# Three-part scores for every head, new instruction sequences, and four expert blocks moved into the last tail of a decoder layer

## What is computed

```python
q = l2norm(xn @ Wq * 16) * 4;  k = l2norm(xn @ Wk) * 4          # 16 heads of q, one of k and v
x = x + layernorm(softmax(q @ k.T) @ v @ Wout)
state = state * exp(d_t * A) + (d_t * u_t) * B_t;  y_t = sum_n state * C_t
x = x + (y + D * u) * silu(layernorm(x))
for e in range(32):                                             # combine is 0 where e is not used
    g, u = split(xl @ w_gu[e].T);  out += (silu(g) * u) @ w_d[e].T * combine[:, e]
```

## Time and profile before

| | |
|---|---|
| time of the runs | 1514.94 us median of 3 (1511.84 to 1518.72) |
| the profiled execution | 1499.86 us, span 1498.1 us |
| mean granted PE clock | 0.952 of full speed |
| PE / DVE / ACT / POOL busy | 1351.0 / 1098.7 / 936.0 / 475.0 us |
| expert blocks run | 68 |

### The profile page before, as it was taken

How to read it: one execution, slowest core, us unless ns; L and a number is a source line. 1 busy time by engine, 2 the same in 40 slices (tenths; PEclk the granted TensorE clock), 3 DMA queues, 4 the chain that set the end, 5 groups by cost and what they waited for, 6 DMA issues and landing times.

```text
span 1498.1 us, 26182 instructions
## 1 busy us (share of the span) xinstructions
PE 1351.0 (90%) x6762; PEld 992.1 (66%) x6763; DVE 1098.7 (73%) x1513; ACT 936.0 (62%) x2454; POOL 475.0 (32%) x367
## 2 busy tenths in 40 slices
PE   5699899999999999999999999999943779999996
PEld 4367686546888664678865467876422667888885
DVE  3377589849888995988898598887877446766763
ACT  4658785447878645787864578776320446666663
POOL 0000010000021331331133133163412776766674
PEclk9799999989999999999999999999975789999998
DMA  7459997704788771468777136868812469998883
GB/s 237 170 172 260 276 241 179 190 17 115 171 239 200 188 184 36 115 172 240 197 188 187 36 108 170 248 144 207 215 26 91 105 138 236 228 229 222 231 193 53
DMA packets 137515, 256.80 MB, mean 171 GB/s; under 512 B 48717, under 2 KB 50206, under 8 KB 129104
## 3 DMA queue, kind: packets, MB, share of 16 engines
q0 software_dynamic: 36480, 122.30, 36.9%
q1 hardware_dynamic: 76704, 86.70, 19.9%
q10 hardware_dynamic: 24240, 46.68, 9.9%
HBM read 166.37 MB, written 46.21 MB: 142 GB/s over the span
## 4 chain that ended last, share of the span: by engine, by line
PE 61%; DVE 10%; issue 9%; DMA 9%; ACT 6%; DVEq 1%; POOL 1%; ACTq 1%; SPq 1%; POOLq 0%
PE bank L670 12%; PE bank L693 10%; PE bank L653 6%; DMA out<-y_ring,add_ids 3%; PE bank L537 3%; PE pair L614 3%; PE pair L616 3%; PE pair L615 3%; PE pair L537 3%; PE bank L1161 2%; DMA c_bc<-bc_dram 2%; PE bank L655 2%; PE bank L1163 2%; PE bank L1162 2%; DMA y<-state 2%
## 5 line engine op out<-in xcount | busy, mean ns | idle before, releaser
L670 PEld LDWEIGHTS bank<-v_aug,probs 128*128 128x128 f32 x2048 | 237.1, 191 | 22.2 <-ACT probs L1350 16.7
L670 PE MATMUL bank<-v_aug,probs 128*128 128x129 f32 x2048 | 244.2, 275 | 5.1 <-ACT probs L1350 5.1
L2830 POOL DMA_INDIRECT lists<-entry,slot x128 | 199.8, 1561 | 131.7 <-DVE slot L2320 93.9
L693 PE MATMUL bank<-wout,o_t 128*128 128x512 f32 x512 | 233.3, 611 | 5.1 <-issue 4.3
L1359 ACT ACTIVATE decay<-delta,neg_a 128x511 f32<-128x511 f32 x256 | 165.2, 720 | 50.4 <-DVE dbu L2144 31.3
L1350 ACT ACTIVATE probs<-bank 128x512 f32<-128x512 f32 x256 | 153.0, 608 | 63.0 <-PE bank L670 37.6
L693 PEld LDWEIGHTS bank<-wout,o_t 128*128 128x128 f32 x512 | 98.5, 196 | 125.3 <-issue 125.1
L2845 POOL DMA_DIRECT2D y<-dbu x32 | 28.6, 894 | 380.5 <-DVE dbu L2149 271.6
L2144 DVE TENSOR_TENSOR_SCAN dbu<-decay,dbu 128x1024 f32<-128x1024 f32 x64 | 144.6, 2281 | 4.9 <-ACT decay L1359 2.8
L2144 DVE TENSOR_TENSOR_SCAN state<-decay,state 128x1024 f32<-128x1024 f32 x64 | 145.3, 2284 | 2.5
L2939 POOL DMA_INDIRECT out<-y_ring,add_ids x68 | 119.9, 1763 | 77.0 <-DMA out<-y_ring,add_ids 42.2
(11 more groups left out here) (242 smaller groups left out, 2844.7 us busy)
## 6 DMA issues: line engine op xcount, KB each, us to landing
y<-dbu POOLq DMA_DIRECT2D x32, 1024.0 KB
w_raw<-in_w_exp ACTq DMA_DIRECT2D x64, 512.0 KB
wq<-wq_dram POOLq DMA_DIRECT2D x30, 1024.0 KB, 8.6
y<-state POOLq DMA_DIRECT2D x28, 1024.0 KB
wout<-in_wout SPq DMA_DIRECT2D x64, 256.0 KB, 5.0
b_bc<-bc_dram SPq DMA_DIRECT2D x64, 256.0 KB, 4.1
c_bc<-bc_dram SPq DMA_DIRECT2D x64, 256.0 KB, 5.2
lists<-in_const ACTq DMA_DIRECT2D x3, 2904.0 KB, 13.7
```

The lines of the kernel that those rows point to most:

```text
L670: mm = pe.matmul(bank_o[half][:, (t % 2) * (DH + 1):(t % 2 + 1) * (DH + 1)], probs[:, k, t * P:(t + 1) * P], v_aug[:, k, :], start=(k == 0 ...
L693: mm = pe.matmul((bank_o + bank_s)[t][:], o_t[:, h, t * P:(t + 1) * P], wout[:, h % 4, :], start=(h == 0), stop=(h == H - 1))
L2830: pool.indirect_dma_start(out=lists, out_offset=bass.IndirectOffsetOnAxis(ap=slot[:, t, k:k + 1].bitcast(U32), axis=0), in_=entry[:, t, :] ...
```

## The change

There are three parts.

1. Every head is scored in three f32r matmuls. `q_t` and `k_t` are gone, `q_hi` and `q_lo` hold four heads, and DVE makes `q_lo` for each head.
2. The written sequences of all streams in the rows are new: the same calls, with 32 more `q_lows`, in another order.
3. Lists of experts 0 to 3 have their first block closed behind the third row (if fewer than 128 tokens are in it by then, the count is filled up). These four blocks are numbered 0 to 3, the second blocks of the same experts follow from block 4. SP loads their ids (`lists_first`) and POOL gathers their tokens (`get_first`) when `out_proj` of row 3 is done. PE, ACT and DVE work through them by calls written out between the router, the counting steps and the loop. POOL interleaves row 3's sends with the adds and gathers of blocks 0 to 13. Experts 0 and 1, and 2 and 3, then share a loop (`two_experts`), since their remaining blocks count together.

```diff
-                if j < 2:
-                    pe.wait_ge(S["qT_ok"], r * H + h + 1)
-                else:
-                    pe.wait_ge(S["klo_ok"], r + 1)
-                    pe.wait_ge(S["qlo_ok"], r * G * 2 + g * 2 + (j - 1))
+                pe.wait_ge(S["klo_ok"], r + 1)
+                pe.wait_ge(S["qlo_ok"], r * H + h + 1)
...
-                if j < 2:
-                    mm = pe.matmul(bank_s[k % 2][:], k_t[:, tile], q_t[:, j, :], start=True, stop=True)
-                else:
-                    pe.matmul(bank_s[k % 2][:], k_hi[:, tile], q_hi[:, j - 2, :], start=True, stop=False)
-                    pe.matmul(bank_s[k % 2][:], k_lo[:, tile], q_hi[:, j - 2, :], start=False, stop=False)
-                    mm = pe.matmul(bank_s[k % 2][:], k_hi[:, tile], q_lo[:, j - 2, :], start=False, stop=True)
+                pe.matmul(bank_s[k % 2][:], k_hi[:, tile], q_hi[:, j, :], start=True, stop=False)
+                pe.matmul(bank_s[k % 2][:], k_lo[:, tile], q_hi[:, j, :], start=False, stop=False)
+                mm = pe.matmul(bank_s[k % 2][:], k_hi[:, tile], q_lo[:, j, :], start=False, stop=True)
...
-                act.activation(k_t[:], bank_t[1][:], ACT.Copy).then_inc(S["kT_ok"], 1)
...
+            def lists_first():
+
+                sp.wait_ge(S["op_ps"], NB * TT)
+                sp.wait_ge(S["sent"], (NB - 1) * SENT)
+                for r in range(PRE):
+                    load_get(0, r, r * CAP)
+                    load_add(r, r * CAP)
...
+                pe.wait_ge(S["lgs_ok"], NB)
+                gate_up(0, 0, 0)
                 ranks(b)
+                ht(0)
+                counts()
+                down(0, 0)
+                xt(0, 2)
+                table_rows()
+                gate_up(1, 1, 1)
+                ht(1)
...
+                load_expert(3)
                 gates(b)
                 split_expert(2, 0)
+                split_expert(2, 1)
+                split_expert(3, 0)
+                split_expert(3, 1)
                 norm_seed(b, "f")
-                split_expert(2, 1)
+                xt(0)
+                xt(1)
...
+            xt(2)
+            hidden(1)
+            split(2, 0)
+            split_rest(2)
+            ht(1)
+            hidden(2)
+            xt(3)
+            ht(2)
+            split(3, 0)
+            split_rest(3)
+            hidden(3)
+            ht(3)
...
+            sends(0)
+            pool.wait_ge(S["x2_out"], NB * 16)
+            add_next(0)
+            sends(1)
             pool.wait_ge(S["xf_out"], NB * 16)
+            get_now(4)
+            sends(2)
+            add_next(1)
+            get_now(5)
```

More of the change, by code:

```diff
@@ L42 @@
 QUAD = 4
+PRE = 4
 LIST_COLS = NE + 1
@@ new lines, in counts, with table_rows @@
+            def counts():
+                pe.wait_ge(S["carry_ok"], NB)
+                pe.matmul(cnt_bank[:, 0:NE], ones, carry[:], start=True, stop=True).then_inc(S["cnt_ps"], 1)
+            def table_rows():
+                pe.wait_ge(S["cols_ok"], 1)
+                for i in range(6):
+                    row = bank_t[1][0:1, i * P:(i + 1) * P] if i < 4 else bank_t[0][0:1, (i - 4) * P:(i - 3) * P]
+                    mm = pe.matmul(row, cols_f[:, i:i + 1], ident, start=True, stop=True)
+                mm.then_inc(S["rows_ps"], 1)
@@ L745, in ranks @@
                 pe.matmul(bank_t[0][:, 0:TT * NE], ones, carry[:].unsqueeze(1).to_broadcast([P, TT, NE]), start=False, stop=False)
+                if b == NB - 2:
+                    filled = bank_t[0][:, TT * NE:TT * NE + PRE]
+                    pe.matmul(filled, ones, carry[:, 0:PRE], start=False, stop=False)
+                    for t in range(TT):
+                        pe.matmul(filled, ones, r["act"][:, t, 0:PRE], start=False, stop=False)
                 for t in range(TT - 1):
@@ L1142, in _ @@
-            pe.matmul(ht_bank[:, 0:NE], ones, carry[:], start=True, stop=True).then_inc(S["cnt_ps"], 1)
-            pe.wait_ge(S["cols_ok"], 1)
-            for i in range(6):
-                row = bank_t[1][0:1, i * P:(i + 1) * P] if i < 4 else bank_t[0][0:1, (i - 4) * P:(i - 3) * P]
-                mm = pe.matmul(row, cols_f[:, i:i + 1], ident, start=True, stop=True)
-            mm.then_inc(S["rows_ps"], 1)
-            def xt(q, r):
-                wait_apart(pe, S[f"blk_in{r}"], q * 16 + 16)
-                for k in range(KT):
-                    mm = transpose(pair[:, r % 2, k * P:(k + 1) * P], x_blk[:, r, k * P:(k + 1) * P])
-                mm.then_inc(S["xt_ps"], 1)
@@ L1923, in _, with expert_at, two_experts @@
             act.reg_mov(more_now, more_blocks(act, 0))
-            act.reg_mov(blk_now, 0)
-            xt(0)
-            silu(0)
-            xt(1)
-            def expert(e, splits, loads, last=False):
+            act.reg_mov(blk_now, PRE)
+            xt(4)
+            silu(4)
+            xt(5)
+            def expert_at(blk):
+                return act.value_load(blocks[0:1, bass.ds(blk + B_EXPERT, 1)], min_val=0, max_val=PRE - 1)
+            def two_experts(following, opened):
+                more, c = act.snap(more_now, min_val=MIN_BLK - 1, max_val=2 * EXP_BLK), act.snap(blk_now, min_val=0, max_val=MAX_BLK)
+                ht(c)
+                xt(c + 2)
+                for e in opened[0:1]:
+                    split(e, 0)
+                    split(e, 2)
+                silu(c + 1)
+                for e in opened[0:1]:
+                    split(e, 1)
+                then = more_blocks(act, following)
+                with act.Fori(0, more) as k:
+                    blk = c + k
+                    weigh(blk, expert_at(blk))
+                    ht(blk + 1)
+                    xt(blk + 3)
+                    silu(blk + 2)
+                for e in opened[1:]:
+                    split_expert(e, 0)
+                    split_expert(e, 1)
+                act.reg_mov(more_now, then)
+                act.reg_mov(blk_now, c + more + 1)
+                weigh(c + more, expert_at(c + more))
@@ L1930, in expert @@
+            def expert(e, splits, loads, last=False, opened=()):
                 more, c = act.snap(more_now, min_val=MIN_BLK - 1, max_val=EXP_BLK - 1), act.snap(blk_now, min_val=0, max_val=MAX_BLK)
@@ L2964, in _, with get_now, sends @@
+            def get_now(blk):
+                get_next(-1, blk - 2)
+            def sends(k):
+                send_last(range(k, k + 1))
+            pool.wait_ge(S["op_ps"], NB * TT)
+            pool.memset(x_blk[:], 0.0).then_inc(S["blank_ok"], 1)
+            pool.wait_ge(S["blank_ok"], 1)
+            pool.wait_ge(S["xf_out"], (NB - 1) * 16)
+            for r in range(QUAD):
+                get_first(r)
             pool.wait_ge(S["slot_ok"], NB)
             pool.wait_ge(S["entry_ok"], NB * 2)
-            send_last(range(0, 3))
+            sends(0)
@@ new lines, in _ @@
+            sends(2)
+            add_next(1)
+            get_now(5)
+            sends(3)
+            add_next(2)
+            get_now(6)
+            sends(4)
+            get_now(7)
+            add_next(3)
+            sends(5)
+            get_now(8)
+            get_now(9)
+            add_next(4)
+            sends(6)
+            get_now(10)
+            get_now(11)
+            add_next(5)
+            sends(7)
+            get_now(12)
+            get_now(13)
+            add_next(6)
```

1735 lines of the change are left out of this document (912 added, 823 removed).

## The result

Beside the kernel before on the same chip the changed kernel took 1494.57 us (median of 4 runs, 1490.73 to 1497.15) against 1513.39, a ratio of 0.9875 (95% interval 0.984 to 0.9909), or -18.8 us. In a second comparison, of 12 runs, it took 1500.62 against 1507.75, a ratio of 0.9941 (0.9906 to 0.9977), or -9 us (the two medians alone differ by 7.1). The two intervals only just overlap. The middle of the two is a ratio of 0.991, or -14 us. The profiled execution of after took 1492.85 us (span 1491.1), that of before 1499.86, and of this pair the difference is 7.0 us. Executions of one kernel differ by more than that, so a place is read from the traces and a size from the timed runs.

What follows compares the result with a forecast made beforehand. It took PE to bound the rows (874.6 of 900 us busy) and the experts, and DVE's chain the tail. Rows -21, sequences 0 and early blocks -10 gave -31 us, 1514.9 to 1484 us, range 1469 to 1502.

Steps and rivals of the forecast that it cites:

- rival A: Rows: DVE becomes the bound, so the scores bring 8 us or less instead of 21, giving 1497 us; chance 0.15.
- rival B: Tail: POOL's queue makes blocks 4 to 11 wait as long as now, part 3 brings 0, giving 1494 us; chance 0.16.
- PE's 7 us per row: Scores in the rows: three f32r matmuls save PE 0.22 us per call over 128 calls, 28 us in all.
- the net of -21: Rows: of PE's 28 us, 4 are lost at row 3's end and 3 to new small waits, leaving -21 us.
- so about 19 remain: DVE in a row: about 31 us of slack, less 7 for the shorter row and 5.4 of new `q_lows`.
- Part 2, at 0: New sequences in the rows: the same calls, taken as 0 beyond part 1; at most PE's 25 idle us to win.
- Rival C: Rows: added `q_lo` stand behind scan pieces while PE waits, making the kernel slower, +42 us, 1557 us; chance 0.06.
- Part 3, -10 us: Tail and experts: four early blocks bring -12.7 us, less +1.4 for late gates and +1.3 for expert openings.
- So this queue sets when the blocks up to 10 can run: POOL's queue in the tail: its shortening brings the gather of block 10 12.7 us earlier, at 59.0 us after 1147.7.
- The term of +1.4: ACT in the tail: three weight-load issues ahead of `gates` take 1.44 us and delay what is queued behind them.
- the openings: Blocks 8 to 10: splitting weights of experts 4, 5 and 6 leaves DVE no slack against PE, costing +1.3 us.
- the three signs: Wrong if `x_blk`/`w_lo` waits in blocks 4 to 11 exceed 8 us, gates slip over 2, or `out_stats` waits for scan.

Runs made afterwards that it cites:

- order_only: The kernel before with only the new sequences of the first row and rows 0 to 2, scoring as before: 0.9953 of before, 1501.02 us.
- rows_new: The kernel before with part 1 and the new sequences of the first row and rows 0 to 2, last row, tail and experts unchanged: 0.9897 of before, 1492.04 us.
- the nine profiles: Profiles of nine kernels, after among them, with the same code for the first row and rows 1 and 2: row 1 took 260.0 to 265.5 us.
- the cut sends: The changed kernel, and before with only the new rows, each without 9 of row 3's 32 sends: 0.9816 and 0.9776 of before.
- spread: The changed kernel with shared-expert loops written out and experts 4, 5 and 6 opened one by one: 0.9919 of before, 1498.97 us.
- after_again: The changed kernel run once more beside the partial kernels on the same chip: 0.9941 of before, 1500.62 us.
- straight: The changed kernel with the loops of `two_experts` on ACT and DVE written out for this routing: 0.9898 of before, 1495.16 us.
- rows_last: The changed kernel without part 3, all new sequences kept, including the last row's: 0.992 of before, 1497.89 us.
- two_parts: The changed kernel without the third matmul of each score call, `q_lo` still computed: 0.9808 of before, 1483.18 us.
- cut_after: The changed kernel without 9 of row 3's 32 sends and their list entries: 0.9816 of before, 1482.76 us.
- double_qlo: The changed kernel with each of the 32 added `q_lo` computed twice on DVE: 0.9991 of before, 1509.31 us.
- scores_only: The kernel before with part 1 in before's sequences, added `q_lows` placed by hand and `key_lo` moved ahead: 1.024 of before, 1542.5 us.

## Why the prediction was only partly right

The direction and the range held, the size did not: -31 us forecast, some -14 measured. That the range held was partly luck. Rivals A and B came true together. By my own prices that is 1514.9 - 8 = 1507, outside the range that I gave. The 7 us below it came from a term that I had put at nothing, the new order.

**Part 1, PE's 7 us per row: right.** PE's busy time fell by 7.2 us in row 0 (`order_only` to `rows_new`) and by 7.2 and 4.2 in rows 1 and 2 (before to after). The granted clock was 0.98 and 0.99 in these two rows of before, 0.99 and 0.98 in after, so the 7.2 of row 1 are read a little high and the 4.2 of row 2 low.

**Part 1, the net of -21: wrong, rival A, and this is the first step that failed.** From `order_only` to `rows_new` part 1 brought 8 us (known to some 8), which is what rival A gave it. The step is "so about 19 remain. DVE's new work is therefore covered, but only by slack that is scattered." I had counted only the softplus wait (17.5 us) as fixed and the other 31 us of DVE's idle time as slack. The runs show that some 37 us per row are not to be had, even with 14.7 us less for PE. Before had 45, so only about 8 were there, and the added `q_lo` took some 4 to 5 of them. Row 0 gave its 7 us, and rows 1 and 2 gave 4.2 and 0.8, with the order's small share in it. Row 3 and the tail gave less than nothing: from the `scan_in` of row 3 to the first send before took 1147.68 - 823.9 = 323.8 us, after 1133.52 - 806.5 = 327.0, and in the nine profiles of the same rows 322.0 to 333.9. I had warned that DVE would be late there and took 4 us off. The wait for PE's `out_proj` went from 5.9 to 0.9 us, so it is the scan's stream that now ends last there.

**Part 2, at 0: wrong by 7 us alone, and by far more as a step.** The orders filled row 0's idle time (-5.5 us to the first `scan_in`, ratio 0.9953, interval 0.9917 to 0.999). And part 1 is a loss of 36 us in before's order. The two parts can't be costed one at a time. Rival C named such a loss and I gave it 0.06 because the new order was there to prevent it. That reason was sound, but then the order is worth what it prevents. The other reason, that PE never waited over 1.1 us for anything in the rows of before, was a misreading of the earlier trace rows. The 1.1 us belong to the largest group alone, and the views of the same window have single waits of up to 1.8 us:

```profile
PE bank L653 <- ACT probs L1350: 2.0, 2, 1.8
```

**Part 3, -10 us: wrong, rival B.** The step that failed is "So this queue sets when the blocks up to 10 can run", as I used it. The queue has a hand in the pace, as the cut sends show (as far as their lighter blocks don't explain it). But I followed it only to the gather of block 10 and forecast 59.0 us behind the first send; it came at 65.6. The sum had one wait in it, 2.4 us at the gather of block 4. There were two large ones, 5.3 us there and 4.8 at the add of block 4. And I took a gain at that point for a gain of the run. The queue as a whole still held 32 sends and 8 adds, only four gathers had left it, and its waits rose: idle time before sends, gathers and adds, without the wait for the slots, is 9.5 + 8.8 + 11.7 = 30.0 us, against 9.5 + 6.6 + 6.1 = 22.2. Adds now stand between more of the sends, and one of them, of block 4, waits 4.8 us for its ids. I had also let the early blocks fit into PE's idle time ahead of the table, where only the first of them ran. So the add of block 7 stayed at 85.0 (83.2), and from there both kernels have 60 blocks to go. The rest of the span is this number times the pitch: (1484.31 - 1218.52) / 60 = 4.43 us in after. The term of +1.4 for `load_expert(3)` ahead of `gates` was right. ACT in after, the issues and the first instruction of `gates`, which stood directly behind the same step in before:

```profile
1095.66 1.44 ACTq L1439 DMA_DIRECT2D w_raw<-in_w_exp  x3
1097.13 1.28 ACT L1423 ACT_TABLE_LOAD   x1 [1.33 <-issue]
```

`rows_new`, with before's ACT order there, reached the first send at 1133.51, no earlier than after, but its router's matmuls ran at a granted clock of 0.50 and took 6.9 us, against 3.8 at 0.93 in after. For the openings I had +1.3. `spread`, which takes them apart, won nothing, so no run shows this term.

**What I had said would make me wrong.** Of the three signs one came up clearly: `out_stats` hardly waits for PE any more. The gates start 1.3 us later behind the weight loads, within the 2 us. PE's waits for `x_blk` and `w_lo` from block 4 on are 0.9 us in after (1167 to 1272 us) and 8.3 us in `after_again` (1174 to 1274 us), just over the limit of 8. The sign was badly chosen. The waits for `w_lo` came earlier, at the early blocks (7.4 us in after), and behind them PE waited for other things: for `ht_lo` 8.5 us in after, 1.7 in before (1180 to 1285 us). Of what I had expected to see, the row windows were to be 5 to 7 us shorter each, the gather of block 10 some 11 us earlier and four `down` ahead of the table. They were 4.2 and 0.8, 6.2, and one.

**What stays open.** In the profiles of after, `straight` and `rows_last`, and less so of `spread`, `two_parts` and `cut_after`, ACT stands idle for 4 to 8 us several times among blocks 4 to 10, with nothing of this kernel in the trace to wait for (in after between 1176 and 1217 us); in those of `after_again` and `rows_new` it doesn't. It comes with before's tail too, so it isn't part 3's. The Trainium skill, Runtime: NRT & Kernel Launch, section Instruction fetch mechanics, says that a taken branch out of the fetched window stalls an engine. The code without loops had the idle time all the same, and only one packet of each instruction queue lies between 1176 and 1217 us in after, so these runs don't bear out that cause. The cause stays open, and so does that of the lower clock behind block 7.

## What to carry to other kernels

Idle time of an engine isn't slack until something has used it. Take work away from the engine that is called the bound, and add some to the next: here 59 us less on PE brought 15, 21 more on DVE cost 12, and with the windows of single rows that showed whose chain set the pace. Count the instructions that an edit really takes out, in the trace. Cost an edit together with the order that it needs, since the same calls gained 16 us in one order and lost 36 in another. And where a queue feeds a stretch, compare where the whole queue ends, not where one of its items comes; here work that was taken out behind it was worth nothing, with the queue as it was and with 12 us less in it.

## What the hardware did that I had not expected

PE's time in a row hangs on the granted clock by more than the change: row 2 ran at a granted clock of 0.99 in `order_only` and 0.97 in `rows_new`. Its PE time went from 257.1 to 254.5 us; times the clock it is 254.5 against 246.9, so 7.6 us less work left 2.6 us less time. The length of a row goes with the clock as well. Among the nine profiles of the same row code, row 1 took 260.0 to 260.6 us in the four with a mean granted clock of 0.987, 262.1 and 262.6 in the two with 0.974, and 265.5 in the one with 0.968. So the clock's share has to be taken off before two rows are compared. `two_parts`, with 14.7 us less work for PE per row, ran its rows at 0.974 and 0.961, and over its six runs at a mean of 0.942 against 0.949 in those of after. The lower clock may have eaten part of the saving. No run shows that, and `double_qlo`, with all of PE's work, had 0.943 too.

And the pitch of the last 48 blocks (from the add of block 19 to that of block 67), where all these kernels run the same loops, varied from profile to profile: 4.33 us in before, 4.35 in `rows_new`, 4.48 in `scores_only`, 4.34 and 4.47 in two executions of after. Between these two that is 6 us over 48 blocks. The granted clock doesn't explain it (0.990 in the slow `scores_only`, 0.986 in `rows_new`). That is as large as half of the effect under study, and why single profiles could not settle part 3.
